# Masked keys replaced by the mean of the unmasked ones in the first stage of a decoder layer; no mask products in attention

## What is computed

```python
x = x0 + linear_attention(layer_norm(x0)); x = x + gelu(layer_norm(x) @ w1 + b1) @ w2 + b2
# cross attention, 16 heads of 8 channels, 77 keys
attn = einsum('bhtd,bhnd->bhtn', q, k) * scale
attn = softmax(where(key_padding_mask, -inf, attn)); x = x + (attn @ v) @ Wo.T + bo
# 8 experts, top 2, limited capacity, gated FFN
```

## Time and profile before

| what | value |
|---|---|
| median of 3 runs | 1022.3 us (1021.0 to 1023.09) |
| profiled execution: its time | 1019.92 us |
| its span, first to last instruction | 1017.9 us |
| mean granted PE clock | 0.958 |
| busy, share of span | PE 88%, PEld 62%, DVE 58%, ACT 46%, POOL 51% |

### The profile page before, as it was taken

How to read it: one execution, slowest core, us unless ns; L and a number is a source line. 1 busy time by engine, 2 the same in 40 slices (tenths; PEclk the granted TensorE clock), 3 DMA queues, 4 the chain that set the end, 5 groups by cost and what they waited for, 6 DMA issues and landing times.

```text
span 1017.9 us, 26993 instructions
## 1 busy us (share of the span) xinstructions
PE 896.1 (88%) x9394; PEld 631.8 (62%) x9394; DVE 589.0 (58%) x1890; ACT 468.8 (46%) x721; POOL 515.3 (51%) x715
## 2 busy tenths in 40 slices
PE   3699999999999999999999999998349999999960
PEld 1577777776666666666666666666226767667650
DVE  5677777777556676667666766765402222344436
ACT  1256566566445555455555555545123434334320
POOL 4334444454422255555555555555626666666670
PEclk9799999999999999999999999999669999999995
DMA  4369500000000000000000001000021333245408
GB/s 124 104 239 339 191 0 0 0 1 1 7 8 8 8 30 23 29 21 19 12 16 14 15 15 29 9 10 11 16 84 51 102 89 108 80 138 166 147 25 330
DMA packets 49912, 66.68 MB, mean 66 GB/s; under 512 B 12662, under 2 KB 27813, under 8 KB 49824
## 3 DMA queue, kind: packets, MB, share of 16 engines
q1 hardware_dynamic: 38448, 52.14, 15.9%
q0 software_dynamic: 9216, 8.42, 2.8%
q10 hardware_dynamic: 2160, 4.86, 1.2%
HBM read 33.83 MB, written 42.09 MB: 75 GB/s over the span
## 4 chain that ended last, share of the span: by engine, by line
PE 57%; DVE 9%; issue 6%; POOL 2%; DMA 2%; ACT 1%; DVEq 1%; POOLq 0%; SPq 0%; ACTq 0%
PE psum L1677 13%; PE psum L1223 7%; PE psum L1689 7%; PE psum L1260 5%; PE psum L1240 4%; DVE Kb L911 2%; PE psum L1671 2%; PE psum L1273 2%; PE psum L1282 2%; PE psum L1210 2%; DVE Y L1603 2%; PE psum L1226 1%; PE psum L1268 1%; PE psum L594 1%; PE psum L1294 1%
## 5 line engine op out<-in xcount | busy, mean ns | idle before, releaser
L1571 POOL DMA_INDIRECT expert_out<-yo,token x160 | 156.2, 976 | 89.2 <-issue 70.8
L1135 ACT ACTIVATE PT<-psum,key_bias 77x2048 f32<-77x2048 f32 x64 | 125.7, 1964 | 131.1 <-PE psum L1243 131.0
L819 POOL DMA_INDIRECT dispatched<-z,idx x128 | 129.0, 1008 | 84.8 <-issue 42.4
L1614 DVE TENSOR_TENSOR h<-psum,act_g 128x512 f32<-128x512 f32 x80 | 55.3, 692 | 150.7 <-PE psum L1677 150.7
L894 DVE TENSOR_REDUCE top_score<-psum 128x8 f32<-128x616 f32 x128 | 101.9, 796 | 62.1 <-PE psum L1226 60.1
L1223 PE MATMUL psum<-Kb,qT 32*128 32x308 f32 x512 | 100.7, 469 | 0.0
L1649 ACT ACTIVATE act_g<-psum 128x512 f32<-128x512 f32 x80 | 47.8, 597 | 89.2 <-PE psum L1677 89.2
L1240 PE MATMUL psum<-qT,Kb 32*77 32x128 f32 x2048 | 86.1, 283 | 0.0
L1689 PE MATMUL psum<-down,h 128*128 128x128 f32 x640 | 78.1, 275 | 0.8 <-DVE h L1614 0.8
L1677 PE MATMUL psum<-xT,gate 128*128 128x512 f32 (+1 forms) x192 | 77.1, 532 | 0.8 <-ACT xT L1634 0.8
L1689 PEld LDWEIGHTS psum<-down,h 128*128 128x128 f32 x640 | 74.7, 192 | 2.1 <-DVE h L1614 1.7
(11 more groups left out here) (163 smaller groups left out, 1726.6 us busy)
## 6 DMA issues: line engine op xcount, KB each, us to landing
dispatched<-zeros SPq DMA_DIRECT2D x40, 258.0 KB, 2.8
xin<-dispatched SPq DMA_DIRECT2D x40, 258.0 KB, 4.2
expert_out<-zeros SPq DMA_DIRECT2D x32, 256.0 KB, 2.0
X<-in_x SPq DMA_DIRECT2D x16, 256.0 KB, 2.7
yb<-expert_out SPq DMA_DIRECT2D x16, 256.0 KB, 4.0
Y<-expert_out SPq DMA_DIRECT2D x7, 512.0 KB, 8.1
out<-Y ACTq DMA_DIRECT2D x7, 512.0 KB, 6.7
expert_out<-yo,token POOLq DMA_INDIRECT x160, 2.2
```

The costliest lines, as they stand in the source:

```text
L819: pool.indirect_dma_start(xg, bass.IndirectOffsetOnAxis(ap=idx[par][:, t, k:k + 1], axis=0), z4[par][:, t, :], None, bounds_check=ROWS - 1 ...
L1135: nc.scalar.activation(PT[j % 2][:], T.rearrange("p a c -> p (a c)"), ACT.Exp, bias=key_bias[:, bass.ds(b, 1)]).then_inc(s["PT_ready"], 1)
L1571: pool.indirect_dma_start(yt[slot], bass.IndirectOffsetOnAxis(ap=token[i][:, t:t + 1], axis=0), yo[i][:, t, :], None, bounds_check=P * B - ...
```

## The change

Masked keys no longer get -3e38 in the scores. Instead their context rows are replaced by the mean of the unmasked rows of the same batch, before keys are projected. The exponential still drops masked keys by its bias.

- The context stays whole in SBUF (`ctx`, 128 x 4928 f32): four DMAs and one for the mask (now all 128 partitions) go out on SP behind the third x group. The loads by group (`cT`) are gone. SP's first load of expert weights waits for the last products that read `ctx`.
- The count of unmasked keys: POOL makes `open_t` in turn -1, PE sums it in turn 0, DVE makes the reciprocal. `mask_t` and `ones` move to the first constants.
- DVE, turn g, after the moments (place "moments"): `mean_of_open(g - 1)`, three instructions.
- POOL, turn g, between x1b and xs (place "biased"): `fill_masked(g - 2)`, three instructions; `residual` is cut in two for it.
- PE: the two products of L1226 in each half are gone, as are `first_row` and `mask_rows`.

```diff
+        later["ctx"] = sb("ctx", [P, B * S2])
...
-                  (block_mask, "block_mask"), (head_mask, "head_mask")]
+                  (block_mask, "block_mask"), (head_mask, "head_mask"), (later["mask_t"], "mask_t"), (later["ones"], "ones")]
...
-            with sp.Fori(1, NG) as g:
+            def load_x(g):
                 sp.wait_ge(s["x_loaded"], 16 * g)
                 sp.dma_start(X[:, bass.ts(g, G4), :], d["x"][:, bass.ts(g, G4), :]).then_inc(s["x_loaded"], 16)
+
+            with sp.Fori(1, 4) as g:
+                load_x(g)
+            for i in range(4):
+                part = slice(i * NG // 4 * G4 * S2, (i + 1) * NG // 4 * G4 * S2)
+                sp.dma_start(later["ctx"][:, part], d["ctxT"][:, part]).then_inc(s["ctx_loaded"], 16)
+            sp.dma_start(later["mask"][:], d["mask"]).then_inc(s["ctx_loaded"], 16)
+            with sp.Fori(4, NG) as g:
+                load_x(g)
 
...
-            sp.wait_ge(s["mask_zeroed"], 1)
-            for q in range(NQ):
-                sp.dma_start(later["mask"][q * ROWS_Q:q * ROWS_Q + 1, :], d["mask"]).then_inc(s["mask_loaded"], 16)
...
-            pool.memset(later["mask"][:], 0).then_inc(s["mask_zeroed"], 1)
...
                 pool.tensor_tensor(x1b[:], x1[:], over(b2_row[:], 1, G4), ALU.add).then_inc(s["x1b_ready"], 1)
+
+            def residual_sum(f):
                 pool.wait_ge(s["x1b_ready"], f + 1)
...
+                between(g, "biased")
+                if group(g - 1):
+                    residual_sum(g - 1)
...
+                between(g, "moments")
...
-        mrow = [sb(f"mrow{i}", [P, G4, S2], BF16) for i in range(2)]
+        mrow = sb("mrow", [P, G4, S2], BF16)
+        kept, filled = sb("kept", [P, G4, S2]), sb("filled", [P, G4, S2])
+        open_count, open_sum, open_mean = sb("open_count", [P, B]), sb("open_sum", [P, G4]), sb("open_mean", [P, G4])
...
-        def sync(sp):
-            def load(g, par):
-                if some(g - 1):
-                    sp.wait_ge(s["v_ps"], g - 1)
-                    sp.wait_ge(s["k_ps"], g - 1)
-                    sp.sem_inc(s["passed"], 1)
-                if some(g):
-                    sp.wait_ge(s["ctx_loaded"], 16 * g)
-                sp.dma_start(cT[par][:], d["ctxT"][:, bass.ts(g, G4 * S2)]).then_inc(s["ctx_loaded"], 16)
-
-            def steps(g, par):
-                if group(g + 2) and some(g + 1):
-                    load(g + 2, par)
-
-            load(0, 0)
-            load(1, 1)
-            groups(sp, steps)
-
...
-            def mask_rows(g, par):
-                if some(g - 1):
-                    pool.wait_ge(s["S_ps"], 4 * G4 * (g - 1))
-                pool.tensor_copy(mrow[par][:].rearrange("p t n -> p (t n)"),
-                                 mask[:, bass.ts(g, G4 * S2)]).then_inc(s["mrow_ready"], 1)
+            def fill_masked(g):
+                pool.tensor_copy(mrow[:].rearrange("p t n -> p (t n)"),
+                                 mask[:, bass.ts(g, G4 * S2)]).then_inc(s["fill_step"], 1)
+                pool.wait_ge(s["fill_step"], 3 * g + 1)
+                pool.wait_ge(s["mean_step"], 3 * g + 3)
+                pool.sem_inc(s["passed"], 1)
+                pool.tensor_tensor(filled[:], mrow[:], over(open_mean[:], 2, S2), ALU.mult).then_inc(s["fill_step"], 1)
+                pool.wait_ge(s["fill_step"], 3 * g + 2)
+                pool.tensor_tensor(c["ctx"][:, bass.ts(g, G4 * S2)], kept[:].rearrange("p t n -> p (t n)"),
+                                   filled[:].rearrange("p t n -> p (t n)"), ALU.add).then_inc(s["fill_step"], 1)
...
-                            mask_rows(g + 1, other)
...
+                if place == "biased" and group(g - 2):
+                    fill_masked(g - 2)
                 if not isinstance(g, int):
                     return
+                if (g, place) == (1, "biased"):
+                    pool.wait_ge(sems["a"]["ctx_loaded"], 16 * 5)
+                if (g, place) == (-1, "biased"):
+                    pool.tensor_scalar(open_t[:], c["mask_t"][:], 0.0, None, ALU.is_equal).then_inc(s["open_step"], 1)
                 if (g, place) == (NG - 3, "end"):
...
-                if (g, place) == (NG - 2, "end"):
-                    mask_rows(0, 0)
...
+            def mean_of_open(g):
+                if some(g):
+                    dve.wait_ge(s["fill_step"], 3 * g)
+                rows = bass.ts(g, G4 * S2)
+                v.scalar_tensor_tensor(kept[:].rearrange("p t n -> p (t n)"), mask[:, rows], 0.0, c["ctx"][:, rows],
+                                       ALU.is_equal, ALU.mult).then_inc(s["mean_step"], 1)
+                dve.wait_ge(s["mean_step"], 3 * g + 1)
+                v.tensor_reduce(open_sum[:], kept[:], AX.X, ALU.add).then_inc(s["mean_step"], 1)
+                dve.wait_ge(s["mean_step"], 3 * g + 2)
+                v.tensor_tensor(open_mean[:], open_sum[:], open_inv[:, bass.ts(g, G4)], ALU.mult).then_inc(s["mean_step"], 1)
...
+                if place == "moments" and group(g - 1):
+                    if isinstance(g, int) and g == 1:
+                        dve.wait_ge(sems["a"]["ctx_loaded"], 16 * 5)
+                    mean_of_open(g - 1)
                 if not isinstance(g, int):
                     return
+                if (g, place) == (0, "moments"):
+                    dve.wait_ge(s["open_step"], 2)
+                    v.tensor_scalar(open_count[:], banks[7][:, 0:B], 1.0, None, ALU.max).then_inc(s["open_step"], 1)
+                    dve.wait_ge(s["open_step"], 3)
+                    v.reciprocal(open_inv[:], open_count[:]).then_inc(s["open_step"], 1)
+                    dve.wait_ge(s["open_step"], 4)
                 if (g, place) == (NG - 3, "end"):
                     ln_stats(0, 3, stat3, xrow)
                     ln_moments(0, 3, stat3, mom3)
...
-            def keys(g, par):
-                pe.wait_ge(s["ctx_loaded"], 16 * g + 16)
-                nc.tensor.matmul(misc[:, 0:G4 * S2], wk[:], cT[par][:], start=True, stop=True).then_inc(s["k_ps"], 1)
+            def keys(g):
+                pe.wait_ge(s["fill_step"], 3 * g + 3)
+                nc.tensor.matmul(misc[:, 0:G4 * S2], wk[:], c["ctx"][:, bass.ts(g, G4 * S2)], start=True, stop=True).then_inc(s["k_ps"], 1)
...
-                    pe.wait_ge(s["mrow_ready"], g + 1)
...
-                    nc.tensor.matmul(S[:, i], qT[par][rows_of(q), j * P:(j + 1) * P], Kb[par][rows_of(q), :, j * S2:(j + 1) * S2], start=True, stop=False)
-                for i in range(2):
-                    q = 2 * half + i
-                    nc.tensor.matmul(S[:, i], first_row[rows_of(q)], over(mrow[par][rows_of(q), j], 1, HB),
-                                     start=False, stop=True).then_inc(s["S_ps"], 1)
+                    nc.tensor.matmul(S[:, i], qT[par][rows_of(q), j * P:(j + 1) * P], Kb[par][rows_of(q), :, j * S2:(j + 1) * S2],
...
+                if (g, place) == (0, "down01"):
+                    pe.wait_ge(s["open_step"], 1)
+                    nc.tensor.matmul(banks[7][:, 0:B], ones[0:S2, :], open_t[:], start=True, stop=True).then_inc(s["open_step"], 1)
...
+            sp.wait_ge(b["k_ps"], NG)
+            sp.wait_ge(b["v_ps"], NG)
...
-        "mask": c(np.asarray(i["mask_BxS2_bf0"]).reshape(1, B * S2)),
+        "mask": rows(i["mask_BxS2_bf0"]),
```

36 lines of the change are left out of this document (16 added, 20 removed).

## The result

The changed kernel takes **1038.2 us** (median of 4 runs, 1030.06 to 1043.64) against 1022.69 for the kernel before, a ratio of 1.0135 [1.0092, 1.0178]. The forecast was 1023.3 with a range up to 1029.0: the change was to cost next to nothing, and by the medians it costs 15.5 us. The profiled execution is the shortest of the four, 1030.06 us with a span of 1028.2 and a mean granted clock of 0.937 (before: 1019.92, 1017.9, 0.958). The three longer ones have 0.928, 0.928 and 0.922, so the clock is the first thing to look at. The changed kernel ran twice more on other chips: 1.0095 [1.0062, 1.0127] and 1.0084 [1.0046, 1.0121]. In the last of these the comparison leaves the longest runs out; its plain median is 1037.95 against 1022.78.

The account below looks back on a forecast made before the run. PE bounds attention (busy 391.4 of 410.0 us); the first stage is tight between DVE and PE. Terms -8.3 + 0 + 3.0 + 4.4 + 1.7 + 0.2 = +1.0 on the 1022.3 median give 1023.3 us, range 1017.0 to 1029.0.

Parts of the forecast that it names:

- Term 1: Attention on PE: 64 removed half-1 pairs save 0.13 us each, -8.3 us; half 0's 64 count 0.
- rival C: Attention: all 128 removed pairs count, -8.3 us more, 1015.0 us; chance 0.06.
- Term 2: First stage, 15 turns: DVE's mean fits into its 1.24 us hole ahead of k, cost 0.
- Term 3: First stage: POOL's fill holds DVE's n, about 0.25 us in each of 12 turns, +3.0 us.
- Rival A: First stage: DVE is not held by POOL's fill, third term 0, 1020.3 us; chance 0.20.
- rival B: First stage: DVE becomes the bound, turns 0.6 us longer instead of 0.25, +5.2, 1027.5 us; chance 0.20.
- Terms 4 and 5: Hand-over to attention: PE waits for POOL's split behind the fill, +4.4 us; half clock behind it, +1.7 us.
- Term 6: Small ones: the count product in turn 0 ahead of a transposition, +0.2 us; the others 0.

Follow-up runs that it names:

- experiment 7: Kernel before plus one product with overwritten result ahead of the ranks: 0.9969 with the mask products, 0.9908 without them.
- the undone version: Changed kernel with GpSimd's split of batch 0's maxima moved ahead of its fill of group 15: 0.9969 of the kernel before.
- nopairs_4: Kernel before with only its mask products left out, on a chip without stalls: 1034.38 us, 1.0099 of the kernel before.
- best3: Changed kernel with GpSimd's split of batch 0's maxima ahead of the fill, and one overwritten 128-column product ahead of the ranks: 0.9892, again 0.9908.
- best2: As best3, with half 0's pair of products also put back (adding zero) into the changed kernel: 1015.05 us, 0.9922 of the kernel before.

## Why the prediction was wrong

**Term 1, the mask products, -8.3: right in size.** Attention less the clock's share went from 431 to 423, and experiment 7 gives 6.6 to 7.2; half 0's pair is free, as argued from L1231's waits, and rival C is out. (The two ends in the earlier trace rows, 505.23 and 505.35, are 0.12 apart and not 0.13, so the sum is 7.7 by its own rows; the timelines of both kernels give 0.13.)

**Term 2, the mean on DVE, 0: right.** k starts 0.13 behind open_mean's start and X to X is 15.17 us (137.94 to 153.11), against 15.16.

**Term 3, the fill holding n, +3.0: wrong, measured 0.** The hold is real, but n x4 grew by 0.58, not by the 1.4 that "each POOL instruction holds one n" gives. The gaps were taken as 0.07; the trace has 0.26 and 0.18 between cast, product and sum, and DVE gets through. What was left went into the idle 0.97 in front of X. Rival A was right here, and rival B is out. The Trainium skill's "GPSIMD Engine Reference" (Key points) names contention for instructions of DVE with two SBUF inputs; kept agrees faintly, with 0.54 us beside the end of xs against 0.47 alone. Over twelve turns that is 0.8 us of DVE's time, near the 1 us that the prediction gave as the price, but k starts 3.29 us behind X instead of 3.28, so it costs nothing.

**Terms 4 and 5, the hand-over, +4.4 and +1.7: right.** 4.32 us of wait, and 5.44 instead of 3.81 us for the down products, 1.6, with 3.4 us at 0.50; the undone version gives 5.7 for both. **Term 6, +0.2 for the count product**, cannot be seen in "to first X", which varies by 3 us anyway.

**The step that failed is the one that isn't in the sum.** The prediction charged the clock only behind the one stop it foresaw, and wrote that work taken off PE counts. It took attention's clock of 1.00 in the earlier trace rows as given, a term of 0 without a reason, although the work that it took off was part of what kept it there: without the products alone, nopairs_4 has 63.6 us of attention at 0.50, where the kernel before has 3.4 and 10.2 in its two profiles, on other chips without stalls. Half 0's pair was "set at 0" as hidden by a wait; nothing was said of what that work did for PE's clock. The rows held a warning: behind the stretch with 2.32 of 3.40 us busy the clock fell at once. They do not say how near attention was to it, and no rival of the prediction had the clock fall in attention. The range names "a low clock of 7 to 10 us", without a place or a row for it, and 1023.3 with 7 more is already past its end of 1029.0. The terms of the sum come to -8 + 0 + 0 + 5.7, some -2 us; 39 us more at 0.50 in attention at 0.4 each are +15.5 in the profiled execution, which with its start 2.5 us earlier comes near the 10.3 by which the spans differ; the other executions, with a lower clock, lose more.

**Open.** Why the mask products, put back, leave three falls on the chips with stalls, and whether they would bring back the clock on the others; what the stalls are; and why executions of one kernel differ so much (clock 0.937 to 0.922 in the first four). The falls lie at fixed places of the group, but not at each passing of them, and PE's longest wait, 0.66 us, is at neither, so more than the place and the idle time must count, perhaps the moment; no run here separates it. The Trainium skill's "TensorE: Matmul & The Clock Gate" (What's actually happening) says that the gate's observation runs free of the kernel, by which the moment would count; the spread of the runs agrees, and nothing here proves it.

## What to carry to other kernels

Before taking "useless" products off a busy TensorE, ask what the granted clock rests on, and price a fall by the rows at 0.50, here 0.4 us for each us. If falls appear, look at what TensorE did ahead of each of them (here row-tiled and narrow products, some next to a wait), and put one product whose result nobody reads into a wait that is there anyway. Here 0.36 us of idle time, filled, was worth 9.7 us on a chip without stalls, and 3 to 6 us on one with them; another filler, the pair of half 0, did little. And read the mean clock of every run, not of the profiled one alone: the profiled run of the changed kernel, its shortest, hid half of the loss.

## What was not expected of the hardware

The clock fell in stretches of attention with PE over 94% busy on the whole and no idle gap above 0.66 us (290 to 700 us of the changed kernel). The Trainium skill ("TensorE: Matmul & The Clock Gate", A second HAM failure mode) tells of short idle times between groups of products that make the clock swing; the traces agree in part: filling gaps of 0.36 us took the falls behind them away, while gaps of 0.66 us had none. Its section "Why this matters for your kernels" asks, against drops in the middle of a kernel, only that long idle gaps between bursts be kept out; by that none of these falls would have come, and here the measurement decides.

Removing the same work gained 0.2 to 0.4% on three chips and cost 1.0% on another. One chip's verdict on an edit of this size isn't every chip's.

The fastest version tried, best3 (the change with the split first and the product at the ranks; 0.9892 and 0.9908), and best2 (0.9922) beat the kernel before. Beside the changed kernel only best2 ran: 1015.05 against 1033.03 on the same chip.
